# Writing the spline's slices into y instead of adding them: x's slices gathered in the main pass

## The reference, cut to what matters

```python
h = gru(cond_2048, x)                       # (4, 1024, 1024), sequential in time
xf = layernorm(h) * gamma + beta
tile_idx = route(sign(xf))                  # one of 64 slices for each token
x_slice = take_along_axis(xf, tok_dims)     # its 16 elements
u = clip((x_slice - mn) / (mx - mn + 1e-8)) # mn, mx: over all tokens of the same slice
delta = (base[...] + slope[...] * x_local) * output_scale[tile_idx]
y = x + h + zeros.at[tokens, tok_dims].set(delta)
```

## Time and profile before

| | us |
|---|---|
| median of three runs (2509.69 to 2511.22) | 2510.69 |
| the profiled execution | 2510.37 |
| its span | 2508.6 |
| PE busy | 2354.8 (94%) |
| DVE busy | 1301.2 (52%) |
| ACT busy | 661.4 (26%) |
| POOL busy | 190.5 (8%) |

### The profile page before, as it was taken

The page is one execution under the profiler, slowest core; times in us unless marked ns, Lnnn a source line. Parts: engine busy times, 40 slices in busy tenths (PEclk is TensorE's granted clock), DMA queues, the critical chain, the costliest instruction groups (busy, mean ns, idle before and its releaser), DMA issues. The chain is left out here.

```text
span 2508.6 us, 83678 instructions
## 1 busy us (share of the span) xinstructions
PE 2354.8 (94%) x35300; PEld 1294.4 (52%) x35300; DVE 1301.2 (52%) x2682; ACT 661.4 (26%) x1333; POOL 190.5 (8%) x376
## 2 busy tenths in 40 slices
PE   7999999999999989999999999999999999977734
PEld 3444444444444444555666666666666666544411
DVE  4322121212123357676666655666666666888865
ACT  2200000000001223333333333333333333355510
POOL 0000000000000000000000000111111111122217
PEclk9999999999999999999999999999999999999955
DMA  6594131313132455443444444444444444477712
GB/s 213 166 345 163 51 126 51 126 52 129 51 143 101 151 156 153 138 150 116 136 135 135 135 127 111 118 117 117 117 116 117 115 116 119 128 228 233 219 43 4
DMA packets 179894, 330.33 MB, mean 132 GB/s; under 512 B 27856, under 2 KB 89728, under 8 KB 178752
## 3 DMA queue, kind: packets, MB, share of 16 engines
q1 hardware_dynamic: 145360, 267.53, 33.7%
q10 hardware_dynamic: 24192, 44.05, 4.7%
q0 software_dynamic: 10240, 17.31, 4.7%
HBM read 222.13 MB, written 156.77 MB: 151 GB/s over the span
## 5 line engine op out<-in xcount | busy, mean ns | idle before, releaser
L573 PE MATMUL rz_bank<-w_hi,hi 128*32 128x512 f16 x6912 | 422.7, 387 | 52.9 <-DVE hi L869 36.7
L308 DVE SCALAR_TENSOR_TENSOR out_stage<-acc,bias_row 128x512 f32<-128x512 f32 x168 | 116.2, 691 | 629.0 <-PE acc L364 629.0
L362 PE MATMUL acc<-w_hi,x_even 128*128 128x512 f16 x768 | 293.3, 382 | 17.8 <-DVE x_even L300 11.3
L573 PEld LDWEIGHTS rz_bank<-w_hi,hi 128*32 128x32 f16 x6912 | 177.9, 98 | 231.6 <-DVE hi L869 44.8
L363 PE MATMUL acc<-w_hi,x_even 128*128 128x512 f16 x768 | 293.1, 382 | 0.0
L364 PE MATMUL acc<-w_lo,x_even 128*128 128x512 f16 x768 | 292.9, 381 | 0.0
L696 ACT ACTIVATE rz<-sums 128x512 f32<-128x512 f32 x176 | 111.1, 631 | 541.2 <-DVE sums L834 540.9
L834 DVE SCALAR_TENSOR_TENSOR sums<-rz_bank,stage 128x512 f32<-128x512 f32 x176 | 121.5, 690 | 244.9 <-PE rz_bank L573 244.8
L573 PE MATMUL rz_bank<-w_lo,hi 128*32 128x512 f16 x4096 | 243.4, 379 | 0.0
L573 PE MATMUL rz_bank<-w_hi,lo 128*32 128x512 f16 x4096 | 243.4, 379 | 0.0
L573 PE MATMUL n_bank<-w_hi,hi 128*32 128x256 f16 x6912 | 234.8, 279 | 0.0
(11 more groups left out here) (191 smaller groups left out, 2665.3 us busy)
## 6 DMA issues: line engine op xcount, KB each, us to landing
stage<-gi_scratch SPq DMA_DIRECT2D x704, 96.0 KB
gi_scratch<-out_stage ACTq DMA_DIRECT2D x168, 256.0 KB, 2.0
stage<-sums_scratch SPq DMA_DIRECT2D x40, 512.0 KB
stage<-in_xT SPq DMA_DIRECT2D x32, 512.0 KB, 6.4
y<-in_x_rows SPq DMA_DIRECT2D x32, 512.0 KB, 4.4
hs_scratch<-h SPq DMA_DIRECT2D x128, 128.0 KB
x_keep<-hs_scratch SPq DMA_DIRECT2D x32, 512.0 KB, 3.9
y<-hs_scratch POOLq DMA_DIRECT2D x32, 512.0 KB
```

The lines of the kernel that those rows point to most:

```text
L308: nc.vector.scalar_tensor_tensor(out=out_stage[:, tb], in0=acc[e % BANKS][:], scalar=UNSCALE, in1=bias_row[:].rearrange("p q f -> p (q f)" ...
L362: nc.tensor.matmul(acc[e % BANKS][:], hi, wh, start=k == 0, stop=False)
L573: last = nc.tensor.matmul(bank[q * COLS:(q + 1) * COLS, 0:b - a], state[:, s, j], w[:, j, q * QW + a:q * QW + b], start=first and j == 0, ...
```

## The change

For each tile, `pool_keep` now issues two gathers in a row, the second with the same row numbers from x in DRAM into `x_now`, a piece of the same scratch room. Both count on the semaphore `picked`, which `pool_pick` now awaits at 32 for each tile. `pool_pick` adds the two into a new tile `base` and then copies `pick_now` as before. In the spline DVE adds `base` to `delta` after the multiplication, as a second instruction of each group, and POOL's 32 indirect DMAs write the result to y without accumulating. `records` now lies in the room of `picks`, and `delta` in that of `rise`. `begin_y` and `pool_add`, which put x + h into all of y, stay.

```diff
+    x_now = out_room[:, at + 8 * NT:at + 8 * NT + SLICE]
+    base = t["base"]
...
-            pool.indirect_dma_start(out=pick_now[:], out_offset=None,
-                                    in_=hs_dram.rearrange("i q p (k j) -> (i q p k) j", j=SLICE),
-                                    in_offset=bass.IndirectOffsetOnAxis(ap=row_now[:, 0:1], axis=0)).then_inc(picked, 16)
+            for now, rows in ((pick_now, hs_dram), (x_now, x_rows)):
+                pool.indirect_dma_start(out=now[:], out_offset=None,
+                                        in_=rows.rearrange("i q p (k j) -> (i q p k) j", j=SLICE),
+                                        in_offset=bass.IndirectOffsetOnAxis(ap=row_now[:, 0:1], axis=0)).then_inc(picked, 16)
 
         def pool_pick(pool, T, tile):
-            pool.wait_ge(picked, T * 16)
+            pool.wait_ge(picked, T * 32)
             pool.sem_inc(wait_carrier, 1)
+            nc.gpsimd.tensor_tensor(base[:, one(tile)].rearrange("p o j -> p (o j)"), x_now[:], pick_now[:], ALU.add)
             nc.gpsimd.tensor_copy(t["picks"][:, one(tile)].rearrange("p o j -> p (o j)"), pick_now[:]).then_inc(pick_kept, 1)
...
-    delta = sb("delta", [P, TILES, SLICE])
+    delta = rise
...
-                nc.vector.tensor_tensor(delta[:, s], value[:, s], wide(per_tok[:, s, 0]), ALU.mult).then_inc(delta_ready, 1)
+                step(nc.vector.tensor_tensor(delta[:, s], value[:, s], wide(per_tok[:, s, 0]), ALU.mult))
+                nc.vector.tensor_tensor(delta[:, s], t["base"][:, s], delta[:, s], ALU.add).then_inc(delta_ready, 1)
...
                     pool.indirect_dma_start(out=y_slices[:], out_offset=bass.IndirectOffsetOnAxis(ap=row_i[:, i:i + 1], axis=0),
-                                            in_=delta[:, i], in_offset=None, compute_op=ALU.add).then_inc(added, 16)
+                                            in_=delta[:, i], in_offset=None).then_inc(added, 16)
...
+        t["base"] = ctx.enter_context(nc.sbuf_tensor("base", [P, TILES, SLICE], F32))
...
-        t["records"] = ctx.enter_context(nc.sbuf_tensor("records", [P, TILES, SLICE], F32))
+        t["records"] = t["picks"]
```

## The result

In what follows a comparison is a set of kernels timed one after the other on one chip, the kernel before always among them. In the first one the changed kernel took **2498.79 us** (median of 5, 2498.2 to 2503.03), the kernel before 2510.41 (median of 5). In four later comparisons the same two kernels were timed again: 2499.41 (2511.41 before), 2500.03 (2510.11), and then twice about 2521 (2510.02 and 2510.81). Until there, all figures of the changed kernel are of comparisons without these stops, except where a_fourth is named. Groups of tiles in the spline are counted from 0, as in the prediction.

A forecast was written before the change was run, and what follows sets the result against it. POOL's issuing of the spline's scatters was taken to bound the kernel; 11.1 us saved there, 0 in the loop and 3.0 paid at the recurrence's end gave -8.1, so 2502.6 us, range 2500.0 to 2508.8.

The forecast's parts named there:

- What bounds the kernel: Spline's end: POOL's time for issuing scatters is the kernel's time, 28 x 1.855 = 51.9 us.
- The scatter's price: Spline: a plain scatter issues in 1.10 us, like the gather, instead of 1.554; 11.1 us saved.
- The bound of 0.894: Spline: lowest price for issuing a plain scatter, from the quickest direct DMA; then 13.6 us saved.
- Its reason: Spline's scatters: accumulating ones are dear because handled row by row, 128 data packets; plain ones lack this.
- The rule on "small, variable" descriptor generation: Spline: by this page, plain scatters stay at 1.554 us to issue; rival of unchanged price, 2514.2 us, chance 0.15.
- DVE's additions: Spline: each group's extra addition takes 0.26 or 0.24 us with gap; the second delta comes 0.5 us later.
- The loop: Loop over tiles: the second gather's 1.4 us on POOL is hidden, by 0.15 to 0.26 us in short tiles; cost 0.
- The short tiles slip: Rival, loop: a second gather's slot of 2.35 us costs ten short tiles 0.6 us each; 2508.6 us, chance 0.08.
- The end of the recurrence: After the loop: second gathers delay shift by 1.4 us and the last pick by 1.6; cost 3.0 us, bounds 1.6 to 4.0.
- The 4.6 us behind the last scatter: From the last scatter's issue to the span's end: no change taken, the packets being few either way.
- The sum: Whole kernel: -11.1 us from scatters + 3.0 at the recurrence's end = -8.1 us, giving 2502.6 us; forecast chance 0.70.
- The range's lower end: Whole kernel: 2500.0 us; the 0.894 us scatter's 13.6 saved, with 3.0 paid, gives 2500.1.

The follow-up runs named there:

- a_fourth: The changed kernel unaltered, timed again in a later comparison where PE stopped 39 times: 2520.8 us, before 2510.02.
- e1: The kernel before with only the accumulation left out of its 32 scatters, so x + h is missing from the slices: 2496.57 us, before 2511.41.
- e3: The changed kernel with its two gathers exchanged, x first, then the states: 2499.51 us, ratio 0.9954.
- e10: The kernel before with accumulating scatters of only 64 of each tile's 128 rows: 2506.0 us, before 2511.05.
- e11: The kernel before with plain, not accumulating, scatters of only 64 of each tile's 128 rows: 2498.81 us, before 2511.05.
- e6: The changed kernel without DVE's nine additions of base in the spline: 2498.71 us in a single execution.
- e5_again: Second run of the changed kernel with a third, unused gather from x in each tile, without PE's stops: 2512.58 us, before 2510.48.
- a_again: The changed kernel unaltered, timed and profiled a second time: 2499.41 us, ratio 0.9953.
- a_third: The changed kernel unaltered, timed and profiled a third time, without PE's stops: 2500.03 us, ratio 0.9957.
- e4: The changed kernel with x's gather issued after POOL's operations for shift and picks copied before waiting for x's rows: 2497.17 us, later 2500.13 and 2498.07.
- e7: The changed kernel with pool_add's direct DMAs writing the states into y instead of adding them: 2498.78 us in a single execution.

## Why the prediction was right and wrong, point by point

**What bounds the kernel: right.** POOL's time for issuing a scatter was the stage's time. Dropping the accumulation alone gave 14.8 us (e1).

**The scatter's price: this term failed.** I took the gather's 1.10 us, behind POOL's small operations, as the nearest row; the place of a scatter is behind another scatter, and there both kinds take 0.96 (e3, and the row of L1509). The sum by its own steps with 0.96: group 1's first scatter was put 22.7 us after the spline's first matmul and came at 22.6 (2458.77 - 2436.13); group 5's was put at 43.7 and came at 43.7 (2479.83 - 2436.13). Up to there the price doesn't matter, since POOL waits: 3.54 us, or 3.24 beyond its usual gap, where 1.4 were forecast. The last 14 took 14 x 1.263 - 0.30 = 17.4 us and not 19.3. Saved 13.0 and not 11.1: **1.9 us** of the miss. The bound of 0.894 had held it.

**Its reason: half wrong.** Packets go by rows, POOL's time mostly doesn't: some 0.43 of 0.60 us is fixed for each accumulating DMA (e10, e11). The rule on "small, variable" descriptor generation in the Trainium skill, "DMA: Bandwidth & Descriptors", section "Anatomy of one DMA — SWDGE (gpsimd) path", fails here as a rival: POOL's issue was the bound, and it went from 1.55 to 0.96 us with nothing but the accumulation taken away. Between tiles of equal kind it hardly varied (953 to 1057 ns).

**DVE's additions: right.** 0.5 at group 1 and 0.26 more at group 5 were put down; e6 has 0.9 for all.

**The loop: right where PE doesn't stop.** ACT never waits for `shift` in the tile shown, the loop is 0.1 to 0.5 us longer, and 0.3 us of cover are left (e5_again). "The short tiles slip" is out. That a second gather could cost PE something in the full tiles, where I had found the most room, was in none of my rivals. It is the gravest gap: in two of five comparisons it turned 11 us of gain into 11 of loss, and that the first one had no stops was luck for the forecast's direction.

**The end of the recurrence: right, a little high.** 3.0 forecast; 2.6 in the first trace, 2.0 and 3.0 in a_again and a_third. `shift` came 1.27 us later (1.41), by the same error in the gather's price, and the last pick is what varies.

**The 4.6 us behind the last scatter: wrong by 0.4.** "The packets are few either way" was too quick. In 40 slices of the 4.8 us from 2503.9 in the kernel before and of the 4.5 us from 2497.1 in the changed one, about where the last issue ends, the DMA engines' busy tenths are:

```profile
DMA  0000089950000000000000000000000000000000
```
```profile
DMA  0000002000000000000000000000000000000000
```

144 packets are moved by about 1.0 us after the issue, 32 by about 0.7, and the rest of the span is 4.2 to 4.3 instead of 4.6.

**The sum.** -13.0 + 2.0 to 3.0 + 0.5 - 0.4 gives -10.9 to -9.9 in place of -8.1; a_again and a_third, cut as above, have -9.8 with the first part's 0.1 to 1.1 in it. What lies around the span took 1.5 to 1.6 us instead of 1.8, which is 0.2 more. The medians of the three comparisons without stops differ by 11.6, 12.0 and 10.1. Up to 2 us are thus left between traces and medians. No run takes them apart; single executions of one kernel spread by up to 5 us within a comparison, and a profile holds one. The range's lower end, 2500.0, was the sum with the cheapest scatter and the full 3.0 for the end of the recurrence, and had nothing for that spread or for a cheaper end; 1.6 instead of 3.0 there was among my own bounds, and would have put it at 2498.7.

## What to carry to other kernels

Where an engine that issues DMAs is the bound, look at the kind of DMA before its size: an accumulating one cost POOL 0.34 us more as a direct and 0.60 more as an indirect one (of the latter most whatever the rows), and gathering the base early and adding on chip took that out of the stage that ends last. Take the price of an added or altered DMA from a row in the same place (behind another DMA, or behind small operations), and compare what a cheaper engine leaves exposed: here DVE's next delta, and from there on only the work after it counts.

Then time a change's new pattern in several comparisons, not in one: two gathers in a row stopped PE in some and not in others, and three of them more. Put apart, behind `shift`, they gave 2497.2 to 2500.1 us in all three, which makes e4 the version to keep, though only one of these was beside a kernel with stops.

## What the runs showed of the hardware that I had not expected

- Issuing an accumulating indirect DMA of 128 rows of 64 B takes POOL 1.55 us, a plain one 0.96; of 64 rows 1.41 and 0.90. A direct one of a tile's 128 rows of 4 KB takes 0.99 and 0.66.
- Accumulating splits the data: 128 packets of one row each (and 16 more) in place of 16 of 512 B (and 16 small).
- The same gather takes 1.12 us behind small operations and 0.96 directly behind another DMA, with 0.30 us between two DMAs; x's gather behind POOL's `shift` takes 1.06 (e4), and so does the first one in e7.
- PE's instruction stream can stop for 0.6 us, twice, while POOL issues an indirect DMA directly behind another: some 40 times in the full tiles, in three of seven comparisons and on two chips, with no wait that the profile names. The stops begin 0.02 to 0.15 and 0.75 to 0.83 us after the start of the second one's issue.
- The last tile's second gather takes 1.56 us to issue in the changed kernel, where the others take 0.96 (1.62 and 1.06 in e4). That is unexplained.
- Behind the same 3.79 us of idle PE the granted clock stays at 1.00 in some executions and falls to 0.50 for 3 to 7 us in others, which costs 2.5 us where it is longest.
